# The expert stage of a two-layer kernel as one stream of 320 tiles in eight units, with one signal of TensorE for each tile

## The reference, cut to what matters

```
x = x + _L1_ffn_ref(_layernorm(x), ...)          # 8192 tokens

for _ in range(LOOPS):                           # 2
    z_norm = _rmsnorm(z, norm_w)
    logits = z_norm @ router_w                   # 128 -> 8
    scores = softmax(logits)
    topk_vals, topk_idx = top_k(scores, TOP_K)   # 2 of 8
    topk_vals = topk_vals / (sum(topk_vals) + EPS)
    cw = sum(one_hot(topk_idx, E) * topk_vals[..., None], axis=-2)
    for e in range(E):                           # D 128, F 256
        mixed = mixed + flat_cw[:, e:e+1] * swiglu(flat_z, w1[e], w3[e], w2[e])
    z = z + mixed
```

## Time and profile before

| | |
|---|---|
| median of 3 runs | 2765.62 us (2760.9 to 2770.4) |
| profiled execution, time | 2763.83 us |
| its span, first to last instruction | 2762.0 us |
| mean granted clock of PE | 0.878 of 2.4 GHz |
| busy: PE, DVE, ACT, POOL | 2091.5, 1933.9, 1501.0, 1224.7 us |
| first and second layer's attention, integer SwiGLU between | up to 1801 us |
| expert stage | 1801 to 2762 us |

### The profile page before, as it was taken

The page is one execution under the profiler, slowest core; times in us unless marked ns, Lnnn a source line. Parts: engine busy times, 40 slices in busy tenths (PEclk is TensorE's granted clock), DMA queues, the critical chain, the costliest instruction groups (busy, mean ns, idle before and its releaser), DMA issues. The chain is left out here.

```text
span 2762.0 us, 46692 instructions
## 1 busy us (share of the span) xinstructions
PE 2091.5 (76%) x13376; PEld 917.7 (33%) x13376; DVE 1933.9 (70%) x6441; ACT 1501.0 (54%) x3516; POOL 1224.7 (44%) x1732
## 2 busy tenths in 40 slices
PE   1699999999878847889988889821895895976920
PEld 0122222222215533333333333211563563653610
DVE  6599999999967736777787776565674664763512
ACT  0288888888872215676667675600563552653610
POOL 1424334343200025565656564336244766755444
PEclk9999999999999966997899896955997997997965
DMA  3434243443300013424242424011232333323421
GB/s 77 92 70 90 51 93 63 78 74 68 70 2 1 1 31 62 94 55 87 48 92 50 93 49 87 8 65 50 79 97 73 103 98 87 111 84 101 126 59 53
DMA packets 193673, 191.38 MB, mean 69 GB/s; under 512 B 29456, under 2 KB 179088, under 8 KB 187280
## 3 DMA queue, kind: packets, MB, share of 16 engines
q1 hardware_dynamic: 126240, 131.63, 22.9%
q0 software_dynamic: 16384, 33.59, 4.2%
q10 hardware_dynamic: 50800, 23.16, 2.9%
HBM read 94.44 MB, written 92.27 MB: 68 GB/s over the span
## 5 line engine op out<-in xcount | busy, mean ns | idle before, releaser
L586 ACT ACTIVATE l_PT<-l_ps 128x512 f32<-128x512 f32 (+3 forms) x2048 | 944.6, 519 | 354.5 <-PE l_ps L471 339.4
L459 PE MATMUL l_ps<-KT,QT 48*128 48x512 bf16 (+3 forms) x2048 | 586.0, 364 | 146.2 <-DVE l_nmax L661 55.6
L661 DVE TENSOR_REDUCE l_nmax<-l_ps 128x1 f32<-128x512 f32 x1024 | 639.1, 683 | 80.1 <-PE l_ps L459 78.9
L471 PE MATMUL l_ps<-QT,KT 64*128 64x512 bf16 (+3 forms) x2048 | 627.4, 360 | 3.9 <-ACT l_PT L586 3.6
L657 DVE CUSTOM_DVE_ANT_0 l_thrown<-l_ps,mask 128x128 bf16<-128x128 f32 (+3 forms) x1024 | 456.6, 487 | 185.4 <-PE l_ps L459 174.9
L487 PE MATMUL l_ps<-l_PT,vv 128*32 128x512 f32 (+3 forms) x4096 | 488.6, 552 | 6.3 <-ACT l_OT L592 2.5
L459 PEld LDWEIGHTS l_ps<-KT,QT 48*128 48x128 bf16 x2048 | 143.1, 95 | 719.6 <-DVE l_nmax L661 388.6
L1102 PE MATMUL moe_ps<-moe_w,moe_xinT 128*128 x576 | 314.8, 630 | 0.0
L1278 POOL DMA_INDIRECT rows_in<-moe_rows,moe_scat_idx x256 | 250.1, 977 | 82.8 <-issue 82.8
L1265 POOL DMA_INDIRECT moe_yg<-rows_out,moe_gat_idx x256 | 242.6, 948 | 82.0 <-issue 80.9
L779 POOL TENSOR_SCALAR_AFFINE_SELECT l_PT<-l_PT 128x512 f32<-128x512 f32 x256 | 159.4, 634 | 266.6 <-ACT l_PT L586 266.1
(11 more groups left out here) (236 smaller groups left out, 2977.0 us busy)
## 6 DMA issues: line engine op xcount, KB each, us to landing
l_spread<-l_slots SPq DMA_DIRECT2D x64, 768.0 KB, 7.8
QT<-l_spread SPq DMA_DIRECT2D x64, 384.0 KB, 6.8
KT<-l_spread SPq DMA_DIRECT2D x64, 384.0 KB, 8.7
moe_xin<-rows_in SPq DMA_DIRECT2D x288, 64.0 KB
rows_out<-moe_y ACTq DMA_DIRECT2D x288, 64.0 KB
x<-in_L_attn_x_dram SPq DMA_DIRECT2D x8, 512.0 KB, 7.2
QT<-l_mrows SPq DMA_DIRECT2D x256, 6.0 KB
rows_in<-moe_rows,moe_scat_idx POOLq DMA_INDIRECT x256
```

The source lines that it names most:

```text
L459: mm = pe.matmul(ps[:, ring(S1, u), 0:width(i)], QT[rows, par, pair, i * P:(i + 1) * P], KT[rows, par, pair, 0:width(i)], start=True, stop ...
L471: mm = pe.matmul(ps[:, ring(S2, u), first(i):SEQ], KT[rows, own, pair, i * P:(i + 1) * P], QT[rows, own, pair, first(i):SEQ], start=True, ...
L586: act.activation(PT[:, r % 2, i, j, first(i):SEQ], ps[:, ring(S2, u), first(i):SEQ], ACT.Exp, scale=scale).then_inc(exp_done, 1)
L661: dve.tensor_reduce(to, ps[:, ring(S1, u), 0:width(i)], X_AXIS, ALU.max, negate=True)\
```

## The change

The two halves become eight units of 1, 2, 2, 3 and 3, 2, 2, 1 passes of eight tiles (four for each loop), with 24, 40, 40, 56, 56, 40, 40 and 24 tiles: 320 in all. They follow each other as one stream; step n of the stream gives each engine its share of tile n and of tiles before it, with no drain at a unit's end. Only passes 0 and 1 stand ahead of it. The table `begin` says after which tile a pass starts; its 20 steps spread over 12 tiles in the first loop and 20 in the second. Passes 16 to 23 are only gathers and additions; 21 to 23 stand behind the stream. `make_tables` follows the last step of a unit's last pass, inside the stream. Each unit has a `rows_out` of its own, each loop four `rows_in`, which are filled with zeros during the integer SwiGLU in place of the zero tiles. The rings have eight places, xn and yg three. In a first-loop pass the second normalisation's variance is computed from the first, and the router works on z and is scaled afterwards.

```diff
-    UNITS = 2 * LOOPS
-    RING = 6
-    LAG = 4
+    PARTS = ((1, 2, 2, 3), (3, 2, 2, 1))
+    RING, HELD, LAG = 8, 8, 5
+    begin = {2: 0, 3: 12, 4: 24, 5: 36, 6: 48, 7: 60, 8: 84, 9: 104, 10: 124, 11: 146, 12: 168, 13: 190, 14: 212, 15: 236,
+             16: 262, 17: 272, 18: 282, 19: 292, 20: 302}
+    def sides(n):
+        return [(k, s) for k, at in begin.items() for s in range(STAGES)
+                if at + s * (12 if k < GROUPS else 20) // STAGES == n]
...
+        def run(tile, side):
+            for k in range(EARLY):
+                for s in range(STAGES):
+                    side(k, s)
+            for n in range(N + LAG + 1):
+                tile(n)
+                for k, s in sides(n):
+                    side(k, s)
+            for k in range(EARLY + len(begin), SIDES):
+                for s in range(STAGES):
+                    side(k, s)
...
 PE
+            def tile(n):
+                v = n - 4
+                if is_tile(v):
+                    pe.wait_ge(h_ready, v + 1)
+                    if v >= 1:
+                        pe.wait_ge(h_copied, v)
+                    for c in range(FF // P):
+                        mm = pe.transpose(ps[:, H, c * P:(c + 1) * P], h[:, v % 4, c * P:(c + 1) * P], w["ident"][:, :])
+                v = n - 1
+                if is_tile(v):
+                    pe.wait_ge(x_copied, v + 1)
...
+                    mm = pe.matmul(ps[:, GU[v % 2], :], xinT[:, v % 2, :],
...
+                v = n - LAG
+                if is_tile(v):
+                    pe.wait_ge(h_copied, v + 1)
+                    if v >= 1:
+                        pe.wait_ge(y_ready, v)
...
+                if is_tile(n):
...
+                    mm = pe.transpose(ps[:, X, 0:P], xin[:, n % RING, :], w["ident"][:, :])
+                    pe.reg_load(held[n % HELD], expert_of[0:1, n:n + 1])
+                if n < N + LAG:
+                    mm.then_inc(step_done, 1)
 ACT
+            def tile(n):
+                if n < N + LAG:
+                    act.wait_ge(step_done, n + 1)
+                if is_tile(n):
+                    act.activation(xinT[:, n % 2, :], ps[:, X, 0:P], ACT.Copy, scale=w["norm_w"][:, 0:1])\
+                       .then_inc(x_copied, 1)
+                v = n - 4
+                if is_tile(v):
+                    act.activation(hT[:, v % 2, :], ps[:, H, 0:FF], ACT.Copy).then_inc(h_copied, 1)
+                v = n - 1
+                if is_tile(v):
...
+                    act.activation(sg[:, v % 2, :], ps[:, GU[v % 2], 0:FF], ACT.Silu).then_inc(sg_ready, 1)
 DVE
+            def tile(n):
+                v = n - LAG
+                if is_tile(v):
+                    dve.wait_ge(step_done, n + 1)
...
+                    dve.tensor_copy(y[:, v % RING, :], ps[:, Y, 0:DIM]).then_inc(y_ready, 1)
+                v = n - 1
+                if is_tile(v):
+                    dve.wait_ge(sg_ready, v + 1)
+                    dve.tensor_tensor(h[:, v % 4, :], ps[:, GU[v % 2], FF:2 * FF], sg[:, v % 2, :], ALU.mult)\
+                       .then_inc(h_ready, 1)
 POOL
+            for k in range(GROUPS):
+                scatter(k)
+            gather(GROUPS)
+            gather(GROUPS + 1)
+            for k in range(GROUPS, 2 * GROUPS):
+                if k + 2 < 2 * GROUPS:
+                    gather(k + 2)
+                scatter(k)
+            for k in range(2 * GROUPS, 3 * GROUPS):
+                gather(k)
 SP, in the integer SwiGLU
+            for rows in rows_in:
+                whole = rows.rearrange("(p r) d -> p (r d)", p=P).rearrange("p (r n) -> p r n", n=512)
+                sp.dma_start(whole, blank[:, :].unsqueeze(1).to_broadcast([P, whole.shape[1], 512])).then_inc(zeroed, 16)
```

More of the change, by code:

```diff
@@ L1021, in experts, with tiles_of, is_tile @@
         sel_ready, k_made = sem("sel_ready"), sem("k_made")
-        rows_ready, scat_ready = sem("rows_ready"), sem("scat_ready")
-        tables, padded = sem("tables"), sem("padded")
+        scat_ready, tables = sem("scat_ready"), sem("tables")
         x_done, out_done = sem("x_done"), sem("out_done")
[L1027 to L1048, removed]
+        side_chain = sem("side_chain")
+        def tiles_of(k):
+            return IT * (k % GROUPS)
+        def run(tile, side):
[9 more added lines that the diff above has]
+                    side(k, s)
+        def is_tile(v):
+            return 0 <= v < N
         block = ctx.enter_context(nc.Block())
@@ new lines, in side @@
+            def side(k, s):
+                if not routes(k):
+                    return
+                if s == 5:
+                    if gathers(k):
+                        pe.wait_ge(added, k - GROUPS + 1)
+                    else:
+                        pe.wait_ge(z_ready, k + 1)
+                    if k >= 1:
+                        pe.wait_ge(t_used, 2 * k)
+                    for t in range(IT):
+                        mm = pe.transpose(psT[:, t * P:(t + 1) * P], z[:, tiles_of(k) + t, :], w["ident"][:, :])
+                        if t % 4 == 3:
+                            mm.then_inc(t_made, 1)
+                if s == 7:
+                    pe.wait_ge(t_used, 2 * k + 2)
+                    if k >= 1:
+                        pe.wait_ge(scat_ready, k)
+                    for t in range(IT):
+                        mm = pe.matmul(psR[:, t, :], zT[:, t * P:(t + 1) * P], w["router"][:, :], start=True, stop=True)
+                    mm.then_inc(r_made, 1)
+                if s == 14:
+                    pe.wait_ge(sel_ready, k + 1)
+                    pe.matmul(psK, upper[:, :], selb[:, :, :], start=True, stop=False)
+                    for t in range(IT):
+                        mm = pe.matmul(psK[:, t + 1:, :], ones[:, :],
+                                       selb[:, t, :].unsqueeze(1).to_broadcast([P, IT - t, EXPERTS]),
+                                       start=False, stop=(t == IT - 1))
+                    mm.then_inc(k_made, 1)
@@ L1165, in _ @@
+            run(tile, side)
         @block.scalar
         def _(act):
[L1167 to L1235 removed]
@@ new lines, in gather @@
+            def gather(k):
+                loop, t0, u = k // GROUPS - 1, tiles_of(k), unit_of[k - GROUPS]
+                pool.wait_ge(tables, u + 1)
+                for s in range(RING):
+                    pool.wait_ge(y_stored[s], stored_by(u, s))
+                if k >= GROUPS + 3:
+                    pool.wait_ge(added, k - GROUPS - 2)
+                for a in range(2):
+                    for t in range(IT):
+                        pool.indirect_dma_start(yg[:, k % 3, a, t, :], None, rows_out[u],
+                                                bass.IndirectOffsetOnAxis(ap=gat_idx[:, loop, a, t0 + t:t0 + t + 1], axis=0))\
+                            .then_inc(gathered[k % 3], 16)
@@ L1577, in two_layers @@
         rows = "b (t p) d -> p (b t) d"
+        rows_in = [nc.dram_tensor(f"rows_in{a}", [EXPERTS * 16 * P, DIM], F32, kind="Internal").ap() for a in range(4)]
         with ExitStack() as both:
```

743 lines of the change are left out of this document (294 added, 449 removed).

## The result

| | before | after |
|---|---|---|
| time, median of 4 runs each, one chip | 2767.68 us | 2863.47 us |
| span of the profiled execution | 2762.0 us | 2867.2 us |
| first and last turning of x | 1936.58, 2633.57 | 1845.97, 2822.43 |

Ratio 1.035, 95% interval 1.031 to 1.039: slower; 2903 was forecast. A second comparison gave 2858.17 and 2761.65 us (1.035 again).

A forecast was written before the change was run, and what follows sets the result against it. PE was taken to bound the expert stage, full at 1.64 us a tile. 1851 + 880 + 6 (drain) + 17 + 33 + 33 + 45 + 35 = 2900 for the span, about 2903 us predicted; range 2780 to 3110.

The forecast's parts named there:

- Pace: Tile steps: PE's work and ACT's first two copies alternate instead of overlapping; 2.75 us a step, 880 us for 320 tiles.
- Start: Ahead of the tiles: only two routing passes remain, so the first tile comes at 1851 instead of 1936, minus 85 us.
- Side work: Between tiles, PE waits for routing matmuls (12 and 5 us) and for tables in DVE's row (33 us).
- POOL: Gathers queued behind scatters make DVE, then PE, wait: 25 us lost at pass 16 and 8 at pass 8.
- Clock: PE mostly at 2.4 GHz; nine long waits drop it for three slow steps each, 45 us.
- Rival A: PE's clock stays low in the tile stream for half the tiles or more: 3122 us, up to 3386; chance 0.18.
- the rule on depth-cycling: Skill rule for PE: frequent small pauses between groups of matmuls make the clock swing; it would give Rival A's time.
- End: Behind the last tile: one group is gathered instead of four, 35 us instead of 121.
- Zero fill: During the integer FFN: 33.6 MB of zeros written in 89 us, done before the next layer, costing 0.
- Rival B: In the tile stream ACT's copies still lie under PE's work: 2.15 us a tile, about 2655 us, faster; chance 0.11.
- Rival C: Tile step of 2.60 us, no clock cost, half of the waits hidden: 2769 us, no change; chance 0.07.
- the own family's upper end: Top of the forecast's own span of 2790 to 3020: steps to 2.9, waits to 110, clock to 110; family chance 0.64.

The follow-up runs named there:

- Experiment 1: The changed kernel with the gate and up product taken from tile n-2 and put first in PE's step; 3144.02 us, 1.018 times before on chip 15.
- experiment 2: The changed kernel with ACT copying hT ahead of x; 3222.40 us on chip 15 and 3237.33 us on chip 10, 1.041 times before both times.
- experiment 4: The new stream of 320 tiles with the old order and four signals inside a tile; 3082.67 and 3094.04 us, 0.998 and 0.996 times before.
- experiments 5 and 6: 5: Experiment 1's kernel with the register load moved behind the product, 2703.80 us, 0.978 times before; 6: the candidate, 2556.96 us, 0.927 times before.
- the candidate: The new stream with old order and four signals, gathers ahead of some scatters, tables in four pieces, other last-loop begins, stages two tiles apart; 2556.96 us, 0.927 times before.
- experiment 8: The candidate with one signal for each tile, product n-2 first, register load behind it, hT copied before x; 3093.26 us, 0.998 times before on chip 10.

## Why the prediction was right

1. *Pace.* Right: 880 us forecast, 320 x 2.74 = 877. The loop is 1.10 (forecast 1.07) and PE's own part 1.64, of which only the turning of h (0.25 for 0.22) and the product (0.95 for 0.86) are longer than the 1.53; I had slowed other instructions (among them the down product to the turning of x, 0.54, which came as 0.44), with nearly the same sum; that 2.75 met 2.74 so closely is partly luck. Experiment 1 takes the loop out of PE's way and experiment 2 one copy out of the loop, and the step follows: 1.96 and 2.51; with the old order and its signals it is 1.64 (experiment 4).
2. *Start.* First turning at 1846, forecast 1851. Pass 0 and the first table take 26.3 (1799.26 to 1825.55), forecast 27; the rest is that the stage begins 3.8 earlier than in the earlier trace rows.
3. *Side work.* 50 forecast, 61 came: tables 38 for 33, the rest 23 for 17. (The bound of 48 for tables without slack is 47 by its own terms, 5 + 4 x 6.4 + 2 x 8.)
4. *POOL.* The term that failed: 33 forecast, 16 came. I let seven plain steps pass before DVE asks, but the same stretch holds the table and two low-clock steps, so a part was counted twice: from the last index (2624.84) to the request (2667.39 - 17.31 = 2650.08) it is 25 us, not 19. And scatter and gather took 43 us from that index to the landing (2667.39), not 46. Tile 84 did not wait at all: scatter 7 begins at 2077.98 and DVE asks at 2125.22, 47 us behind, where I took 36 against the 46 that POOL was to need; the table and four low-clock steps lie between.
5. *Clock.* 45 forecast, 26 came: 17 low-clock steps at 1.5 above 2.74, most of 4.26 us (4.4 forecast), where I had 27. They follow the start and the eight long waits, one to four at a time. In stretches without a long wait it was 1.00, as from 2700 to 2822. Rival A fell with that: PE pauses 0.82 us in every step there, and the rule on depth-cycling (the Trainium skill, TensorE: Matmul & The Clock Gate, A second HAM failure mode: psum-queue depth-cycling) did not show here.
6. *End.* 44 forecast from the last turning (a step, 6 and 35), 45 came.
7. *Zero fill.* It took some 90 us (89 forecast) and was over by 915; the DMA share in the integer SwiGLU rose from the earlier trace rows 0.00 to

```profile
825.00:993.00 168.00, 142.08 (x640) 85.41 (x640) 126.04 (x554) 39.41 (x65) 1.23 (x2) 0.97 0.54 201
```

and PE's busy time from 141.24 to 142.08; the expert stage begins no later than before (point 2). It cost nothing.

So the span of 2900 was 33 too high: 5 start, 3 pace, 17 POOL, 19 clock, less 11 side work and 1 end, each rounded. POOL and clock came 36 lower and side work 11 higher, so the whole lies nearer than its terms. The median of the runs lies another 5 under the profiled one (2868.9). Rival B had the right picture for another kernel: with the copies under PE's work the new stream is faster than before (experiments 5 and 6). Rival C fell with the step of 2.74. One bound was added wrongly: the own family's upper end is 1851 + 928 + 6 + 110 + 110 + 35 = 3040 by its terms, not 3020, with no effect on what was measured.

## What to carry to other kernels

Before merging signals, write down the loop: from the last instruction ahead of the signal, through the engine that answers, to the first instruction that needs the answer. If no work of the waiting engine stands in it, the whole loop is added to each step, here 1.10 us on top of 1.64; an instruction that has its input a step earlier, put first, buys most of it back (1.96, and 1.70 with the copies exchanged and the load moved as well). Waits that stand near one another are not added up: the first one pays a part of the next.

## What was not expected of the hardware

On chips 10 and 15 TensorE nearly stands in stretches where POOL issues indirect DMAs back to back; on chip 2 it does not. The stage itself begins alike on all three: the first turning of x stands between 1840 and 1866 in every trace of the new stream. Experiment 4 on chip 10, and the candidate on chip 2:

```profile
2150.00:2175.00 25.00, 4.19 (x9) 1.90 (x9) 0.72 (x2) 1.14 (x3) 18.90 (x21) 0.50 0.22 58
...
2225.00:2250.00 25.00, 25.00 (x151) 17.90 (x150) 19.41 (x85) 15.45 (x44) 0.00 (x0) 1.00 0.26 73
```
```profile
2125.00:2150.00 25.00, 25.00 (x148) 17.71 (x148) 19.61 (x85) 15.51 (x44) 18.91 (x21) 1.00 0.44 126
```

The first is a stretch of pauses. One pause in experiment 8, ACT and DVE:

```profile
2204.34 0.38 ACT L1180 ACTIVATE moe_hT<-moe_ps 128x256 f32<-128x256 f32 x1 [24.28 <-remote]
2204.34 0.29 DVE L1280 COPY moe_y<-moe_ps 128x128 f32<-128x128 f32 x1 [23.83 <-remote]
```

With POOL at 18.90 of 25 us, PE is busy 4.19 on the one and 25.00 on the other; with POOL idle the first has 25.00 too. In the pause both stand 24 us and go on at the same time. By the kernel ACT waits there for nothing but the one signal of PE, whose last turning the trace shows at 2181.00; the profile names no engine as the releaser (`remote`). That the DMAs cause the pauses is inferred from their falling together. Each kernel here issues the same 512 indirect DMAs, and kernels 4 and 8 are at 1.00 on those chips; that the pauses eat their gain is argued too, as neither ran on chip 2. Why the chips differ no run shows: each was used for one group of runs, so chip and hour are not separated.
